# A four-layer graph network on one core: 84 strips of layer 1 are multiplied under layer 0, layer 2's sides are made under layer 1

## The chip, the cores and the metric

The kernel runs on one core of one Trainium2 chip. Its time is the device time of one execution in microseconds. It is written engine by engine: each of TensorE (PE), VectorE (DVE), ScalarE (ACT), GpSimd (POOL) and SyncE (SP, which issues nearly all DMAs) has its own program, runs it in order, and waits for the others by semaphores.

## The reference

Four graph layers over 4096 nodes with 128 features, each followed by a residual sum and a layer norm:

```python
x = _layernorm(x + _L0_gnn_ref(x, adj, W))              # hyperbolic mean: A @ (gamma*XW), A @ (gamma-1), row sums of A
x = _layernorm(x + _L1_gnn_ref(x, adj, W, b))           # D^-1/2 (A+I) D^-1/2 @ x @ W.T + b
x = _layernorm(x + _L2_gnn_ref(t, x, adj, alpha, beta)) # D^-1/2 A D^-1/2 @ x - x
                                                        #   + sigmoid(alpha) * (softmax(beta*cos(x,x)*A) @ x - x)
x = _layernorm(x + _L3_gnn_ref(x, adj, ...))            # relu(A @ x @ W.T + b), then a GRU cell
```

The adjacency A is a dense 4096x4096 fp32 matrix (64 MB), so each layer multiplies it with a matrix of 128 or 129 columns. Layer 2 needs the scores of all pairs of nodes too, with a softmax over each whole row.

## The kernel before, in words

**Tiles.** A is cut into 8 slabs of 512 rows (index s), a slab into 32 strips of 128 columns (index j), two strips make a pair (m, 16 of them), two pairs a group (g, 8 of 1 MB). fp32 products are made of fp16 halves: A's strip and the layer's factor Y are each split in a high and a low part, and three products (high-high, high-low, low-high) are summed in PSUM.

**Layer 0** (`turn0`, `multiply0`, `high0`, `low0`). Each pair of A is loaded in fp32, PE turns it (8 transposes, L525) into one of two strip buffers in PSUM (`strip_a`, `strip_b`), ACT copies the high part (L828), DVE makes the low part (L1352), PE multiplies. Here a quarter strip is the stationary side and Y moves: 130 columns with the low strip (L544), 260 with the high one (L543, L546), for 4 quarters and 2 strips, 16 matmuls a pair. PE turns two pairs ahead of the one that it multiplies, and may turn the next only when the low part of the last but one is made. The split pairs go from a ring of 7 slots back to memory (`adj_t`), from where layers 1 to 3 read them. At a slab's end ACT and DVE read the four sums (`read_acc0`, L834, L835, L1359, L1360), called at pair m == 3 of the next slab. The row work of a slab (`rows0`, some 40 small steps on DVE, ACT and POOL, each waiting for the one before) is spread over the next slab's pairs, steps 2m and 2m+1 at pair m. Layer 1's factor is made from its result (`y_scale` on POOL, `y_high` on ACT, `y_low` on POOL), all in the last slab and behind it.

**Layer 1** (`multiply(1, n)`). The factor is the stationary side and 512 columns of the turned A move, three matmuls of 512 a strip (L567, L568, L574), 6 a pair, 128 pairs in the order of the table TURNS. At a slab's last strip the identity's share, `eye` times a diagonal of 1024, is added (L573). Groups of `adj_t` are loaded into 6 slots in that order. The row work (`rows1`, steps k = 0 to 14, the k-th behind the k-th turn from ROWS_FROM on) ends with x normed to unit length, turned by PE (k == 12) and split into `unit_h`, `unit_l`, the factors of layer 2's scores.

**Layer 2** (`score`, `mask`, `exponentials`, `scale`, `turn2`, `mix`, `multiply2`). A unit is 128 rows by 1024 columns. Its scores take two calls of three matmuls of 512 columns (L612 to L614). A masked product with A and the row's peak take DVE (L1517), which needs the unit of A loaded again from memory (`load_unit`, 25 places in SBUF given by RING). ORDER2 gives the order of units (e = 4 x row block + quarter of the columns). Before slab 0 can be turned (`turn2(0)`, L629), 16 units, the four rows' exponentials on ACT (L897) and their scaling (L903 on ACT, L1549 on DVE) must be done. PEAKS2 and WEIGHTS2 say at which step the first four rows' peaks and weights stand in DVE's program. Two units are multiplied at the end of layer 1, the rest behind it. Units at places from 22 on lie over x (`x_nat`), so their loads wait until Y of layer 2 (`y_high`, `y_low` with L1095 and L1097, and Y_dis, x times a degree factor, L1101) is made for all 8 slabs. **Layer 3** is multiplied like layer 1.

## Time and profile before

| | us |
|---|---|
| three timed runs | 1368.76, 1364.46, 1367.28; median 1367.28 |
| the profiled execution | 1363.03 |
| its span in the trace | 1361.2 |
| PE busy with matmuls | 1245.8 (92%) |
| DVE, ACT, POOL busy | 762.8, 680.2, 483.6 |
| data moved | 413 MB, 303 GB/s over the span |

The page gives busy times per engine and in 40 slices, the chain of waits that ended last, and the costliest groups of instructions. PE's ends are modelled, and weight loads (PEld) lie beside matmuls. A span of PE at 100% in a window means that it waits for nothing; a smaller share has to be read from the timeline.

### The profile page before, as it was taken

What the parts mean: (1) busy time and instruction counts of PE and PEld (TensorE: products, weight loads), DVE (VectorE), ACT (ScalarE), POOL (GpSimd) and SP (SyncE); (2) the same over time, 40 slices, a digit from 0 to 9 for tenths busy, and PEclk for the clock granted to TensorE, in tenths of its full rate; (3) what the DMA queues carried; (4) which work ended last, traced back from release to release, by engine and by line L of the source; (5) the groups of instructions that cost most, each with busy time, mean ns of one, the idle gap of its engine ahead of it and who ended that gap; (6) DMA issues with size and microseconds to landing.
All of it is one profiled execution on the core that took longest, in us unless ns stands there. A gap on an engine that the chain in (4) does not pass through costs nothing.

```text
span 1361.2 us, 20730 instructions
## 1 busy us (share of the span) xinstructions
PE 1245.8 (92%) x7896; PEld 793.4 (58%) x7896; DVE 762.8 (56%) x1716; ACT 680.2 (50%) x983; POOL 483.6 (36%) x459
## 2 busy tenths in 40 slices
PE   5888888888789999986999999999999989999996
PEld 5877777778664555533555555555556554444442
DVE  6755655666551312177778787878878781021223
ACT  5444555445341211154887877887887740112222
POOL 4011221113243321263565666666656571000000
PEclk9899999999899999996999999999999999999998
DMA  9999999999779999936777877778786767987870
GB/s 306 336 415 375 376 387 369 383 386 378 297 279 387 350 362 359 380 139 240 255 263 276 283 275 276 260 262 289 277 284 247 240 245 290 408 309 274 317 283 23
DMA packets 114819, 413.06 MB, mean 303 GB/s; under 512 B 10016, under 2 KB 23584, under 8 KB 90144
## 3 DMA queue, kind: packets, MB, share of 16 engines
q1 hardware_dynamic: 106528, 407.67, 80.7%
q10 hardware_dynamic: 8192, 4.06, 1.0%
q8 instruction: 62, 1.02, 0.3%
q14 instruction: 37, 0.30, 0.1%
HBM read 340.40 MB, written 71.30 MB: 302 GB/s over the span
## 4 chain that ended last, share of the span: by engine, by line
PE 72%; DVE 11%; ACT 6%; POOL 5%; issue 4%; DMA 2%; POOLq 0%; ACTq 0%; DVEq 0%; SPq 0%
PE acc L567 8%; PE acc L568 8%; PE acc L574 8%; PE strip_b L629 8%; PE acc L647 4%; PE acc L644 4%; PE acc L645 4%; PE acc L643 4%; DVE parts L1352 3%; PE strip_b L525 2%; PE strip_a L525 2%; DVE arena L1352 2%; PE strip_a L612 2%; PE strip_a L613 2%; PE strip_a L614 2%
## 5 line engine op out<-in xcount | busy, mean ns | idle before, releaser
L1170 POOL TENSOR_TENSOR parts<-arena,parts 128x512 f16<-128x512 f32 x237 | 275.2, 1170 | 190.0 <-ACT parts L908 186.6
L908 ACT ACTIVATE parts<-arena 128x512 f16<-128x512 f32 x256 | 158.5, 624 | 110.4 <-DVE arena L1558 101.7
L1558 DVE SCALAR_TENSOR_TENSOR arena<-parts,dis,strip_b 128x512 f32<-128x512 f16 x256 | 188.8, 743 | 29.6 <-PE strip_b L629 20.7
L567 PE MATMUL acc<-arena,Y 128*128 128x512 f16 x512 | 194.1, 379 | 3.5 <-DMA arena<-adj_t 2.5
L568 PE MATMUL acc<-arena,Y 128*128 128x512 f16 x512 | 194.1, 379 | 0.0
L574 PE MATMUL acc<-arena,Y 128*128 128x512 f16 x512 | 194.1, 379 | 0.0
L629 PEld LDWEIGHTS strip_b<-ident,arena 128*128 128x128 f32 x1024 | 128.4, 142 | 58.4 <-DVE arena L1558 4.9
L629 PE MATMUL strip_b<-ident,arena 128*128 128x128 f32 x1024 | 155.4, 275 | 7.2 <-ACT arena L903 4.8
L1138 POOL TENSOR_TENSOR sc<-sc,power 128x4 f32<-128x4 f32 x31 | 31.5, 1016 | 324.3 <-DVE sc L1379 324.3
L897 ACT ACTIVATE arena<-arena,neg_peak 128x2048 f32<-128x2048 f32 x64 | 127.3, 1990 | 5.8 <-DVE neg_peak L1528 5.8
L903 ACT ACTIVATE arena<-arena,weight 128x2048 f32<-128x2048 f32 x57 | 113.4, 1989 | 14.0 <-DVE weight L1542 14.0
L1517 DVE CUSTOM_DVE_ANT_0 arena<-strip_a,arena,scal 128x1024 f32<-128x1024 f32 x64 | 82.0, 1281 | 35.1 <-PE strip_a L614 29.3
L647 PE MATMUL acc<-parts,Y 128*128 128x512 f16 x256 | 97.1, 379 | 3.4 <-POOL parts L1170 3.4
L643 PE MATMUL acc<-parts,Y_dis 128*128 128x512 f16 x256 | 97.1, 379 | 0.1
L645 PE MATMUL acc<-parts,Y 128*128 128x512 f16 x256 | 97.0, 379 | 0.0
L644 PE MATMUL acc<-parts,Y 128*128 128x512 f16 x256 | 97.0, 379 | 0.0
L1517 DVE CUSTOM_DVE_ANT_0 arena<-mid,arena,scal 128x1024 f32<-128x1024 f32 x60 | 76.9, 1282 | 35.0 <-PE mid L614 35.0
L525 PE MATMUL strip_a<-ident,arena 128*128 128x128 f32 x512 | 68.9, 279 | 22.6 <-DVE parts L1352 14.4
L567 PEld LDWEIGHTS acc<-arena,Y 128*128 128x128 f16 x512 | 50.1, 98 | 66.5 <-issue 10.2
L568 PEld LDWEIGHTS acc<-arena,Y 128*128 128x128 f16 x512 | 50.1, 98 | 65.4 <-issue 12.6
L525 PE MATMUL strip_b<-ident,arena 128*128 128x128 f32 x512 | 71.2, 284 | 17.3 <-DVE parts L1352 9.8
L574 PEld LDWEIGHTS acc<-arena,Y 128*128 128x128 f16 x512 | 50.1, 98 | 59.5
(321 smaller groups left out, 2398.1 us busy)
## 6 DMA issues: line engine op xcount, KB each, us to landing
arena<-adj_t SPq DMA_DIRECT2D x128, 1024.0 KB, 7.0
arena<-in_adj SPq DMA_DIRECT2D x64, 1024.0 KB, 9.9
arena<-in_adj SPq DMA_DIRECT2D x128, 512.0 KB, 5.7
parts<-adj_t SPq DMA_DIRECT2D x128, 512.0 KB, 6.9
adj_t<-parts SPq DMA_DIRECT2D x37, 1024.0 KB, 8.0
adj_t<-arena SPq DMA_DIRECT2D x27, 1024.0 KB, 8.5
scratch<-v ACTq DMA_DIRECT2D x8, 256.0 KB, 10.4
arena<-scratch SPq DMA_DIRECT2D x8, 256.0 KB, 4.4
```

Source lines behind the costliest of these rows:

```text
L525: last = pe.transpose(strip[n % 2][:, j % 2, P * q:P * (q + 1)], tile[:, j // Q, q, P * (j % Q):P * (j % Q + 1)], ident[:])
L567: pe.matmul(to, Y[:, j, 0:D], high, start=j == 0, stop=False)
L568: pe.matmul(to, Y[:, j, LO:LO + D], high, start=False, stop=False)
L574: last = pe.matmul(to, Y[:, j, 0:D], low, start=False, stop=j == NB - 1)
L629: last = pe.transpose(strip_b[:, b % 2, P * q:P * (q + 1)], unit_in[:, place, P * (j % 8):P * (j % 8 + 1)], ident[:])
L643: pe.matmul(to, Y_dis[:, j, :], kept_slot(b // 2 % KEPT_SLOTS)[:, b % 2, 1, :], start=j == 0, stop=False)
L644: pe.matmul(to, Y[:, j, 0:D], part_h[:, b % 4, :], start=False, stop=False)
L647: pe.matmul(to, Y[:, j, 0:D], part_l[:, b % 4, :], start=False, stop=j == NB - 1).then_inc(product, 1)
L908: act.activation(part_h[:, b % 4, :], mixed[b % G_SLOTS], ACT.Copy).then_inc(high_done, 1)
L1170: pool.tensor_tensor(part_l[:, b % 4, :], mixed[b % G_SLOTS], part_h[:, b % 4, :], ALU.subtract).then_inc(low_done, 1)
L1517: dve.tensor_tensor_reduce(unit_in[:, place, :], flat(scores_at(i)[:]), unit_in[:, place, :], scal[:, 5:6], NEG_HUGE, ALU.mult, ALU.max, p ...
L1558: dve.scalar_tensor_tensor(mixed[b % G_SLOTS], kept_slot(n % KEPT_SLOTS)[:, b % 2, 0, :], dis[:, j:j + 1], strip_b[:, b % 2, :], ALU.mult, ...
```

## The change

1. **Strips ahead.** In layer 0, pair m of slab s is multiplied with layer 1's factor as well when `m // 2 <= s - 2`: 2, 4, ... 12 pairs of slabs 2 to 7, 42 pairs or 84 strips. Y becomes one array of 516 columns: layer 0's low part (0:130) and high part (130:260), layer 1's high (260:388) and low part (388:516). The matmuls of such a pair are 388 and 258 columns wide instead of 260 and 130, and one of 128 is added for each quarter. The additional sums stand in columns 260 to 388 of the same four PSUM banks. `read_acc0` copies them to `turned`, SP stores them (`put_share`, 256 KB a slab) and loads them in layer 1 (`load_share`) over `eye`, where DVE adds the identity's share (`eye_share`, which POOL made before).
2. For that, layer 1's factor of slab s-1 is made at pairs 13 to 15 of slab s. `read_acc0` stands at m == 2, ahead of that pair's split, and the row steps at pair m are 2m+3 and 2m+4.
3. **Layer 1** multiplies the remaining 86 pairs, slabs in the order 0, 1, 6, 7, 4, 5, 2, 3. A slab's row work starts at its end, or 12 turns behind the start of that of the last but one.
4. **Layer 2 under layer 1.** The high part of its factor is made by ACT in each slab's row work, the low part by DVE (`y_low2`). Seven units instead of two are multiplied under layer 1, behind turns 72, 74, ... 84, with the masks at the same steps. ORDER2 takes first the columns whose slabs are done; the last quarter (e % 4 == 1, slabs 2 and 3) comes last, and the peaks of rows 0 to 2 move behind it. Y_dis takes the place of layer 1's high part in Y, so it waits for the end of layer 1.

The core of the diff:

```diff
+Y1H = YW
+Y1L = YW + D
+YC = YW + 2 * D
+YD = YW
+HIGH_AT = [LO, Y1H, 0, 0]
+LOW_AT = [0, Y1L, D, D]
...
+ORDER = {1: [0, 1, 6, 7, 4, 5, 2, 3], 3: list(range(SLABS))}
+FIRST = {1: [2 * max(s - 1, 0) for s in range(SLABS)], 3: [0] * SLABS}
+
+
+def turns(l):
+    return [(s, m) for s in range(2) for m in range(EARLY)] + [(s, m) for s in range(2) for m in range(EARLY, PAIRS)] \
+        + [(s, m) for s in ORDER[l][2:] for m in range(FIRST[l][s], PAIRS)]
+
...
+ENDS1 = [TURNS[1].index((s, PAIRS - 1)) + 1 for s in ORDER[1]]
...
+for at, s in enumerate(ORDER[1]):
+    ROWS_FROM[1][s] = ENDS1[at] if at != 1 else ENDS1[at] + 1
+    if at >= 2:
+        ROWS_FROM[1][s] = max(ENDS1[at], ROWS_FROM[1][ORDER[1][at - 2]] + 12)
+LAST1 = ORDER[1][-1]
...
-ORDER2 = [0, 1, 2, 4, 5, 6, 8, 9, 10, 3, 7, 11, 12, 13, 14, 15] + list(range(16, 4 * NB))
+ORDER2 = [0, 3, 4, 7, 8, 2, 6, 11, 12, 15, 10, 14, 1, 5, 9, 13] + list(range(16, 4 * NB))
+LAST_COLUMNS = 1
...
+EARLY2 = 7
...
-PEAKS2 = {19: 0, 21: 1, 23: 2, 31: 3}
-WEIGHTS2 = {27: 0, 31: 1, 35: 2, 38: 3}
...
+PEAKS2 = {25: 0, 27: 1, 29: 2, 31: 3}
+WEIGHTS2 = {32: 0, 34: 1, 36: 2, 38: 3}
...
+RING = [16, 17, 18, 19, 20, 12, 13, 14, 15, 2, 3, 4, 5, 0, 6, 8, 22, 23, 7, 9, 10, 1, 24, 11, 25]
...
+def early_units(n):
+
+    return [i for i in range(EARLY2) if n == TURNS1 - 14 + 2 * i]
...
+            def put_share(s):
+
+                sp.wait_ge(acc_read, acc_reads_done(0, s))
+                sp.dma_start(share[s], turned[s % 2][:]).then_inc(share_out[s % 2], 16)
+
+            def load_share(s):
+                sp.wait_ge(share_out[s % 2], 16 * (s // 2))
+                sp.wait_ge(product, slab_product(1, two_before1(s)))
+                sp.dma_start(eye[s % 2], share[s]).then_inc(share_in[s % 2], 16)
+
...
+                    if s >= 3 and c == 2:
+                        put_share(s - 1)
...
                 elif place >= 22:
                     sp.wait_ge(y_ready, SLABS * 3)
+                    sp.wait_ge(y_dis_ready, SLABS)
...
+                ahead = m // 2 <= s - 2
+                width = Y1L if ahead else YW
+                if ahead and m % 2 == 0:
+                    pe.wait_ge(y_ready, SLABS + m // 2 + 1)
...
-                            pe.matmul(acc0[q][:, 0:YW], high, Y[:, j, :], start=True, stop=False)
-                        last = pe.matmul(acc0[q][:, 0:LO], low, Y[:, j, 0:LO], start=False, stop=False)
+                            pe.matmul(acc0[q][:, 0:width], high, Y[:, j, 0:width], start=True, stop=False)
+                        last = pe.matmul(acc0[q][:, LO:width], low, Y[:, j, LO:width], start=False, stop=False)
                         if not start:
-                            last = pe.matmul(acc0[q][:, 0:YW], high, Y[:, j, :], start=False, stop=stop)
+                            last = pe.matmul(acc0[q][:, 0:width], high, Y[:, j, 0:width], start=False, stop=stop)
+                        if ahead:
+                            last = pe.matmul(acc0[q][:, Y1H:Y1L], high, Y[:, j, Y1L:YC], start=False, stop=False)
                 last.then_inc(product, 1)
 
...
-                if n in (TURNS_ALL - 4, TURNS_ALL - 2):
-                    for k in range(2):
-                        score(n - (TURNS_ALL - 4) + k)
+                for i in early_units(n):
+                    score(2 * i)
+                    score(2 * i + 1)
+            for n in range(TURNS1, TURNS1 + HOOKS[1]):
+                for k, s in hooks(1, n):
+                    if s != LAST1:
+                        rows1(k, s)
             for n in range(STEPS2):
-                if n == 6:
-                    rows1(2, SLABS - 1)
-                if n == 14:
-                    rows1(12, SLABS - 1)
+                if n == 2 * EARLY2:
+                    rows1(2, LAST1)
+                if n == 23:
+                    rows1(12, LAST1)
...
+                if s >= 2:
+                    if s >= 4:
+                        act.wait_ge(share_out[s % 2], 16 * (s // 2 - 1))
+                    for q in range(2):
+                        last = act.activation(turned[s % 2][:, P * q:P * (q + 1)], acc0[q][:, Y1H:Y1L], ACT.Copy)
+                last.then_inc(acc_read, 1)
...
+                    y_high(2, s)
...
-                if m == 3 and s > 0:
+                if m == 2 and s > 0:
                     read_acc0(s - 1)
                 high0(n)
...
-                    rows0(2 * m, s - 1)
-                    rows0(2 * m + 1, s - 1)
...
+                    rows0(2 * m + 3, s - 1)
+                    rows0(2 * m + 4, s - 1)
+                    if m == 14:
+                        y_high(1, s - 1)
...
+                pool.wait_ge(row[g % 2], row_done(1, g, "ln_out"))
+                pool.wait_ge(product, product_base[2])
+                pool.tensor_tensor(Y[:, rows_, YD:YD + D], x_nat[:, rows_, :], wide(dis_y[:, rows_]),
+                                   ALU.mult).then_inc(y_dis_ready, 1)
...
+                    if m == 13:
+                        y_scale(s - 1)
+                    if m == 15:
+                        y_low(1, s - 1)
...
+            for g in range(GROUPS):
+                y_with_dis(g)
...
-                if 6 <= n < 6 + GROUPS:
-                    y_with_dis(n - 6)
-                    y_low(2, n - 6)
...
+            def y_low2(s):
+                rows_ = slice(Q * s, Q * (s + 1))
+                dve.wait_ge(y_hi, 2 * SLABS + place_in(1, s) + 1)
+                if s == 0:
+                    dve.wait_ge(y_ready, 2 * SLABS)
+                dve.scalar_tensor_tensor(Y[:, rows_, D:2 * D], x_nat[:, rows_, :], Y_SCALE, Y[:, rows_, 0:D],
+                                         ALU.mult, ALU.subtract).then_inc(y_ready, 1)
+
+            def eye_share(s):
+                if place_in(1, s) >= 2:
+                    dve.wait_ge(share_in[s % 2], 16 * (place_in(1, s) // 2))
+                elif s == 0:
+                    dve.wait_ge(row[1], row_done(0, SLABS - 1, "scale"))
+                    dve.tensor_scalar(dcol_a[:], dcol[:], WHOLE, None, ALU.mult).then_inc(dcol_up, 1)
+                    dve.wait_ge(dcol_up, 1)
+                for q in range(Q):
+                    mine, own = Q * s + q, eye[s % 2][:, P * q:P * (q + 1)]
+                    if place_in(1, s) >= 2:
+                        last = dve.scalar_tensor_tensor(own, x_nat[:, mine, :], dcol_a[:, mine:mine + 1], own,
+                                                        ALU.mult, ALU.add)
+                    else:
+                        last = dve.tensor_scalar(own, x_nat[:, mine, :], dcol_a[:, mine:mine + 1], None, ALU.mult)
...
+                if s >= 2:
+                    if s >= 4:
+                        dve.wait_ge(share_out[s % 2], 16 * (s // 2 - 1))
+                    for q in range(2, 4):
+                        last = dve.tensor_copy(turned[s % 2][:, P * q:P * (q + 1)], acc0[q][:, Y1H:Y1L])
+                last.then_inc(acc_read, 1)
...
+            read_acc0(SLABS - 1)
+            for k in range(7, 17):
+                rows0(k, SLABS - 1)
+            eye_share(0)
+            eye_share(1)
+            for k in range(17, 28):
+                rows0(k, SLABS - 1)
...
+                for s in ORDER[1][2:]:
+                    if n == ENDS1[place_in(1, s) - 2] + 3:
+                        eye_share(s)
+                for i in early_units(n):
+                    mask(i)
...
+            for n in range(2 * EARLY2, STEPS2):
+                if n == 2 * EARLY2:
+                    rows1(3, LAST1)
+                    rows1(4, LAST1)
+                if n == 16:
+                    rows1(6, LAST1)
+                if n == 18:
+                    rows1(8, LAST1)
+                if n == 24:
+                    rows1(14, LAST1)
```

In ACT's program, at the start of layer 0's slab 4 (strip_a and strip_b are the turned pairs, acc the sums, turned1 takes the share), the rows before were:

```order
L828 ACTIVATE arena<-strip_a 128x2x512
L828 ACTIVATE arena<-strip_b 128x2x512
L828 ACTIVATE arena<-strip_a 128x2x512
L834 ACTIVATE arena<-acc 128x260
L835 ACTIVATE arena<-acc 128x260
L828 ACTIVATE arena<-strip_b 128x2x512
L828 ACTIVATE arena<-strip_a 128x2x512
L853 ACTIVATE v1,sc1<-t1 128x128 x4
```

and now they are:

```order
L892 ACTIVATE arena<-strip_a 128x2x512
L892 ACTIVATE arena<-strip_b 128x2x512
L898 ACTIVATE arena<-acc 128x260
L899 ACTIVATE arena<-acc 128x260
L904 ACTIVATE turned1<-acc 128x128 x2
L892 ACTIVATE arena<-strip_a 128x2x512
L926 ACTIVATE v1,sc1<-t1 128x128 x4
L892 ACTIVATE arena<-strip_b 128x2x512
L892 ACTIVATE arena<-strip_a 128x2x512
```

Before, the read of the old sums (L834, L835) stood behind the split of the slab's third pair; now it stands ahead of it (L898, L899), with the two copies of the share behind it.

In POOL's program, from the end of layer 1 to the first low part of layer 2 (arena holds x, parts the low parts), the rows before began so, with the last three repeated for eight blocks:

```order
L1164 TENSOR_TENSOR sc<-sc,power 128x4
L1166 TENSOR_TENSOR v<-arena,sc 128x512
L1101 TENSOR_TENSOR Y_dis<-arena,dis_y 128x512
L1095 TENSOR_SCALAR turned<-arena 128x512
L1097 TENSOR_TENSOR Y<-turned,Y 128x4x128
L1101 TENSOR_TENSOR Y_dis<-arena,dis_y 128x512
L1095 TENSOR_SCALAR turned<-arena 128x512
```

and now the whole piece is:

```order
L1201 TENSOR_TENSOR sc<-sc,power 128x4
L1218 TENSOR_TENSOR sc<-sc,power 128x4
L1220 TENSOR_TENSOR v<-arena,sc 128x512
L1163 TENSOR_TENSOR Y<-arena,dis_y 128x4x128 x8
L1224 TENSOR_TENSOR parts<-arena,parts 128x512 x36
```

The eight Y_dis remain, and the scaled copy and the low part of Y are gone from POOL.

In DVE's program, behind the last slab's unit_low (L1509 before, L1586 now; ISA is a mask and the reading of its peak, TENSOR_REDUCE the peak of a row of units), before:

```order
L1517 ISA peak 128x1
L1509 TENSOR_TENSOR arena<-mid,arena 128x512
L1517 ISA arena,peak<-strip_b,arena,scal 128x1024
L1517 ISA peak 128x1
L1517 ISA arena,peak<-strip_a,arena,scal 128x1024
L1517 ISA peak 128x1
L1517 ISA arena,peak<-mid,arena,scal 128x1024
L1517 ISA peak 128x1
L1526 TENSOR_REDUCE row_peak<-peak 128x1
L1528 TENSOR_SCALAR neg_peak<-row_peak 128x1
L1517 ISA arena,peak<-strip_a,arena,scal 128x1024
L1517 ISA peak 128x1
```

and now:

```order
L1594 ISA peak 128x1
L1586 TENSOR_TENSOR arena<-mid,arena 128x512
L1594 ISA arena,peak<-strip_a,arena,scal 128x1024
L1594 ISA peak 128x1
L1603 TENSOR_REDUCE row_peak<-peak 128x1
L1605 TENSOR_SCALAR neg_peak<-row_peak 128x1
L1594 ISA arena,peak<-mid,arena,scal 128x1024
L1594 ISA peak 128x1
L1603 TENSOR_REDUCE row_peak<-peak 128x1
L1605 TENSOR_SCALAR neg_peak<-row_peak 128x1
L1594 ISA arena,peak<-strip_a,arena,scal 128x1024
L1594 ISA peak 128x1
```

Before, three masks (units 7, 8, 9) ran before the first peak, and this stood at unit 9. Now the mask behind unit_low is that of unit 12, the first that needs the last slab's columns, and the peaks of rows 0 to 2 stand behind units 12, 13 and 14.

## Rows read from the trace of the kernel before

**Rows 1.** Windows by stage: busy PE, PEld, DVE, ACT, POOL; clock; DMA; GB/s.
```profile
80.16:125.60 45.44, 38.71 (x384) 35.04 (x385) 26.78 (x66) 22.95 (x42) 7.95 (x10) 0.96 1.03 397
259.90:303.70 43.80, 37.05 (x384) 33.67 (x385) 26.77 (x66) 22.95 (x42) 7.94 (x10) 0.99 1.02 386
353.40:397.40 44.00, 36.95 (x358) 33.51 (x359) 26.72 (x61) 22.43 (x43) 17.75 (x19) 0.92 0.73 283
397.40:583.60 186.20, 185.25 (x934) 94.37 (x933) 38.93 (x180) 28.39 (x70) 50.67 (x50) 1.00 0.96 363
583.60:634.80 51.20, 31.48 (x122) 12.44 (x120) 40.62 (x80) 25.10 (x31) 28.96 (x27) 0.83 0.38 149
```

**Rows 2.** Timeline of PE at a slab's start: start, length, [idle before].
```profile
259.93 0.27 PE L543 MATMUL acc<-Y,arena 128*128 128x260 f16 x1 [3.13 <-DVE arena L1360]
261.26 1.04 PE L525 MATMUL strip_b<-ident,arena 128*128 128x128 f32 x8
263.48 1.04 PE L525 MATMUL strip_a<-ident,arena 128*128 128x128 f32 x8
```

**Rows 3.** Timelines of ACT and of DVE at the same slab's start.
```profile
257.75 0.38 ACT L834 ACTIVATE arena<-acc 128x260 f32<-128x260 f32 x1
...
259.36 0.42 DVE L1360 TENSOR_SCALAR arena<-mid 128x260 f32<-128x260 f32 x1
```

**Rows 4.** Timeline of DVE in one slab, the low splits (L1352), four of sixteen.
```profile
219.60 1.23 DVE L1352 SCALAR_TENSOR_TENSOR arena<-strip_b,arena 128x1024 f16<-128x1024 f32 x1 [4.97 <-ACT arena L828]
...
234.92 1.23 DVE L1352 SCALAR_TENSOR_TENSOR parts<-strip_b,parts 128x1024 f16<-128x1024 f32 x1
...
243.50 1.22 DVE L1352 SCALAR_TENSOR_TENSOR parts<-strip_a,parts 128x1024 f16<-128x1024 f32 x1
...
257.88 1.22 DVE L1352 SCALAR_TENSOR_TENSOR arena<-strip_a,arena 128x1024 f16<-128x1024 f32 x1 [0.99 <-ACT arena L828]
```

**Rows 5.** Timeline of PE at the end of layer 0.
```profile
396.87 0.27 PE L546 MATMUL mid<-Y,parts 128*128 128x260 f16 x1
396.98 0.22 PE L544 MATMUL acc<-Y,parts 128*128 128x130 f16 x1
397.04 0.27 PE L546 MATMUL acc<-Y,parts 128*128 128x260 f16 x1
...
398.76 0.38 PE L567 MATMUL acc<-arena,Y 128*128 128x512 f16 x1 [0.95 <-DVE arena L1360]
398.98 0.38 PE L568 MATMUL acc<-arena,Y 128*128 128x512 f16 x1
```

**Rows 6.** Timelines of POOL and DVE, the last slab's row work.
```profile
593.33 1.04 POOL L1166 TENSOR_TENSOR v<-arena,sc 128x512 f32<-128x512 f32 x1
...
596.74 0.69 DVE L1509 TENSOR_TENSOR arena<-mid,arena 128x512 f16<-128x512 f32 x1
```

**Rows 7.** Timeline of DVE (masks), and two groups of ACT by line.
```profile
601.83 1.28 DVE L1517 CUSTOM_DVE_ANT_0 arena<-strip_a,arena,scal 128x1024 f32<-128x1024 f32 x1
...
603.47 1.28 DVE L1517 CUSTOM_DVE_ANT_0 arena<-mid,arena,scal 128x1024 f32<-128x1024 f32 x1
...
L897 ACT ACTIVATE arena<-arena,neg_peak 128x2048 f32<-128x2048 f32 x64 | 127.3, 1990 | 5.8 <-DVE neg_peak L1528 5.8
...
L828 ACT ACTIVATE parts<-strip_a 128x1024 f16<-128x1024 f32 x37 | 37.6, 1016 | 28.4 <-PE strip_a L525 28.4
```

**Rows 8.** POOL's L1101 by source, then timelines of POOL, DVE and PE.
```profile
L1101 POOL TENSOR_TENSOR Y_dis<-arena,dis_y x8: 1041/1048/2022, 594.3 to 616.1; 128x512 f16<-128x512 f32 x8
...
619.78 1.16 POOL L1097 TENSOR_TENSOR Y<-turned,Y 128x512 f16<-128x512 f32 x1
...
625.01 1.28 DVE L1517 CUSTOM_DVE_ANT_0 arena<-strip_a,arena,scal 128x1024 f32<-128x1024 f32 x1 [5.79 <-DMA arena<-in_adj]
...
628.17 2.48 DVE L1549 TENSOR_SCALAR arena<-arena,weight 128x2048 f32<-128x2048 f32 x2
...
634.79 1.09 PE L629 MATMUL strip_b<-ident,arena 128*128 128x128 f32 x4 [3.58 <-ACT arena L903]
```

More of the change, by code:

```diff
@@ L342, in groups_loaded @@
         def groups_loaded(l, n):
-            before = sum(i % TURNED_SLOTS == n % TURNED_SLOTS for i in range(GROUPS * SLABS)) if l == 3 else 0
+            before = sum(i % TURNED_SLOTS == n % TURNED_SLOTS for i in range(TURNS1 // 2)) if l == 3 else 0
             return 16 * (before + n // TURNED_SLOTS + 1)
@@ L734, in _ @@
                 multiply0(n)
-            for n in range(TURNS_ALL):
+            for n in range(TURNS1):
                 for k, s in hooks(1, n):
@@ L756, in _ @@
                         rows2(m % NB, m // NB - 1)
-            for n in range(TURNS_ALL):
+            for n in range(TURNS3):
                 if n < PAIRS // 2:
@@ L1031, in _ @@
                     y_high(3, (m - 6) % NB // 4)
-            for n in range(TURNS_ALL):
+            for n in range(TURNS3):
                 if n < PAIRS // 2:
@@ L1722, in _ @@
                     rows2(m % NB, m // NB - 1)
-            for n in range(TURNS_ALL):
+            for n in range(TURNS3):
                 if n < PAIRS // 2:
```

236 lines of the change are left out of this document (101 added, 135 removed).

## Prediction

> **What bounds the kernel now.** I read the busy times by stage first [rows 1]. Layer 0 runs to 397.8 us, layer 1 to 583.6, the hand-over into layer 2 to 634.8, and layers 2 and 3 take the rest, which the change leaves as it is apart from places in Y. TensorE (PE) is the engine that all of them have in common, but its limits differ. In layer 1 it is busy for 185.25 of 186.20 us: only fewer matmuls shorten it. In layer 0 a slab lasts 43.8 us or more, and PE has records for 37 of them. In the hand-over PE has 31.5 busy us of 51.2. So I looked next at why PE idles in the last two.
>
> In layer 0 the timeline of PE [rows 2] shows an undisturbed pair: 8 turns and 16 matmuls in 2.22 us (261.26 to 263.48), so 16 pairs are 35.4 us. The other 8.4 us of a 43.8 us slab are in two places. At the slab's start PE waits 3.13 us for the reads of the old sums: ScalarE (ACT) starts its read at 257.75, VectorE (DVE) ends the last of its own at 259.78 [rows 3]. The last product was done a turn (2.22 less 1.33 us of matmuls, 0.9) before PE's wait began at 256.8, so at 255.9. Both engines first wait for the next pair and split it. The rest lies in the row work of the slab before, which holds up the split of strips on DVE, in order. The split of the fourth pair starts at 219.60, that of the third pair of the next slab at 257.88 [rows 4]: 15 pairs in 38.28 us, 5.1 more than 15 times 2.215. By thirds it is 2.0 (219.60 to 234.92, six pairs), 1.9 (to 243.50, three) and 1.1 (to 257.88, six). Slabs of 45.4 us have in addition a stretch at the lower clock behind the 3.13 us wait (granted clock 0.96 in the slab from 80.16, 0.99 in the one from 259.9 [rows 1]). The layer's last matmul ends at 397.81, 0.95 us before layer 1's first [rows 5].
>
> In the hand-over [rows 6 to 8] the last slab's row work takes 13.8 us from 583.6 (unit_low ends at 597.4). Then DVE masks scores at 1.64 us a unit, and from 619.2 it waits: GpSimd (POOL) makes Y_dis and Y's low part for eight blocks until 620.94, only then may units be loaded over x, and DVE goes on at 625.01. Layer 2's first turn is at 634.79.
>
> **Layer 0 after the change.** 42 pairs (84 strips: 2(s-1) pairs of slab s, from 2 to 7) get 384 more moving columns for each of 8 quarter strips. 512 columns go by in 0.215 us (398.76 to 398.98, and over all of layer 1), so this is 0.162 us each, 1.30 us a pair, 54.6 in all. The last matmul of the three has its own weight load and 128 columns. A matmul of 130 columns with its own load takes 0.06 us (396.98 to 397.04 [rows 5]), which is the columns alone, so I add nothing for it. The Trainium skill (TensorE: Matmul & The Clock Gate, Back-to-back issue gap) gives about 81 ns for each matmul of 128 columns in a sustained stream of loads and matmuls, against 54 by columns. By it 336 such matmuls would be 9 us more; the trace does not agree with it, with its 0.06 us.
>
> What hides them: the wait of PE for a strip. Two strip buffers lie between PE and the split, so 1.30 us more of matmuls per pair let DVE fall back 2.6 us before PE feels it. I count a third of the stalls as hidden where its pairs have the added work. Moved by one pair, as the row hooks are, the thirds lie beside products 2 to 6, 7 to 9 and 10 to 12. So hidden are 0, 0, 1.0, 2.0, 2.7, 4.0 and 4.8 us in slabs 1 to 7. The start of a slab: both reads now stand ahead of the next split, as at layer 1's start, where they wait for nothing else and PE idles 0.95 us [rows 5]. The two narrower copies of the share add 0.3 to 0.5, and PE turns a pair meanwhile (0.9). That leaves 0.5 us of the 3.13, and with it goes the stretch at the lower clock. A slab is then 43.8 - 2.6 + 2.6(s-1) - hidden: 41.2, 43.8, 45.4, 47.0, 48.9, 50.2, and 51.5 for the last, which has no start behind it. Slab 0 ends 2.6 us earlier too, at 77.6 instead of 80.16. The seven slabs behind it are 328.0, so layer 0 ends at 405.6 instead of 397.8. For Y1, now made in every slab (two operations of 128x512 on POOL, 1.05 us each by [rows 8], one on ACT), I add 2. Layer 0: +10 us. Bounds: -11 if the 21 us of stalls left go too, +55 if nothing is hidden and the starts stay.
>
> **Layer 1.** 42 pairs of 6 matmuls go: -54.3 us. Ten more score calls of three matmuls come in: +6.5. The transposes of slab 2's unit rows fall behind its end: -0.5; the longer read at its start: +0.5. New waits: the early units' adjacency stands behind the last group in SP's queue, released by product 74 of 86. From release to use one unit took 4.1 us (620.9 to 625.0); with the 1 MB group ahead, at 397 GB/s, 6.7, and the mask 1.3. PE reaches the third early unit 6.1 us after product 74. That is 2 us, and I take 3. Queued behind that mask on DVE are slab 5's unit_low and slab 2's row work, which have four and more turns of slack. The row work now has 12 turns (15.5 us) and the other slab's matmuls, where it takes 10.8 us to the unit on POOL [rows 6], with y_low2 on DVE (0.7, as unit_low of the same size) and the eye share (twice that) added and two slabs interleaved. I take 1 us. The reloads of the share (256 KB) are asked for seven turns ahead (9 us), and DVE needs some 1.4 of these: nothing. The loads need less than before, 43 groups for 64. Layer 1: -44 us, so it ends at about 550 instead of 583.6.
>
> **The hand-over**, from layer 1's end T. Seven units are done instead of two. The row work of the last slab still takes about 14.9 us (13.8 and a mask more between); beneath it go units 7 to 11. Unit 12 needs it: mask at T+16.4, four masks at 1.64 us end at T+23. POOL makes Y_dis alone, 8 times 1.05, from T+10.8: T+19.2, the load 4.1 us more, T+23.3. Y's low part is on DVE under layer 1. Now the exponentials are late: their first row's peak comes at T+18, and eight of 1.99 us [rows 7] end at T+34. On DVE weights and scales (0.7 and 2.5 for a row's two: 628.17 stands 3.16 behind 625.01, two masks and the weights) stand between masks 16, 17 and 18: from T+23, 3.3 + 1.3 + 3.2 + 1.3 + 3.2 + 1.3 + 0.7 and 2.0 for ACT's scale, T+39.5. So the chain over DVE decides, and layer 2's first turn comes after 39.5 instead of 51.2: -12. Bounds: -17, were it the load alone (T+23.3 and the 9.8 us that stood behind it), and 0.
>
> **Sum.** +10 - 44 - 12 = -46. The profiled execution was 1363.0 (span 1361.2 and 1.8 around it), 4.3 below the median of the runs. 1363.0 - 46 + 4.3 = 1321 us. A measurement of this kernel tells 0.3% from no change, 4 us.
>
> **Rivals.**
> The DMA holds layer 0. For: its share is 1.00 and more in slabs at 386 and 397 GB/s [rows 1]. Against: PE waits there for splits, and the longest slabs are now those with most added work. At 397 GB/s 16.8 MB take 42.3 us, so slabs 0 and 1 lose 5 us of their gain and the shares 1: 1327. The Trainium skill (DMA: Bandwidth & Descriptors, Where 436 GB/s comes from) puts HBM's side at about 358 GB/s. By it no slab could be under 46.9 us, and the trace already has 43.8.
>
> Layer 1's row work holds PE. For: eight chains in 56 turns, in pairs 3 turns apart, each engine in order. Against: slack of some 4 us (12 turns of 1.29 and 2.7 of row matmuls, less the 13.8). If two chains go one after the other (27.6 us against 22), PE waits 5.7 us for each of three pairs, 17 in all: 1338.
>
> PE stays at 1.2 GHz in the hand-over. For: its clock was 0.83 there. Nine units at 2.6 us instead of 1.64: +9, 1330.
>
> Short matmuls wait for their weight loads. Against: the 0.06 us of [rows 5]. If each added one took half as long again as its columns (27 ns), 336 of them are 9 us: 1330 too. The skill's figure above would be this case.
>
> The other side: the strip hand-over works one deep. If a pair's turn (0.9), high split (1.0) and low split (1.2) [rows 4, 7] come after, not beside, its matmuls, each of the 42 pairs costs 2.4 us more: +101, 1422, slower. From 1.1 us a pair it decides. Against: with 3.1 us of hand-over the pairs run at 2.22 now, which only two deep allows. And if none of the 54.6 is hidden, the starts stay and layer 2's hand-over keeps its 51 us, the sum is -54 + 6 + 4 + 55 = +11 (1378), slower too, or nothing if half of the starts shrink.
>
> **Chances.** The forecast 0.67, the DMA 0.07, the row work 0.13, the lower clock or slower short matmuls 0.05, no change 0.03, slower 0.05. All but the last two are faster by over 0.3%: 0.92. The range 1307 to 1342 takes in the row work and, below, two thirds of the stalls that I left in layer 0 (21 us).
>
> **What would show it.** In the changed profile: PE's idle before the first matmul of a slab 0.3 to 1 us instead of 3.13; 1.30 us longer pairs at a slab's head and slabs of about 41, 44, 45, 47, 49, 50, 51 us; layer 0's end near 408 us and layer 1's near 550; waits on PE in layer 1 only around the third early unit; DVE not waiting for a load over x after layer 1's end, but on the exponentials or nothing; layer 2's first turn about 40 us after layer 1's end; layers 2 and 3 as long as before (726 us from that turn). It is wrong if slabs 5 to 7 exceed 53 us, or if PE has over 10 us of waits in layer 1.

## The result, and the profile after

The changed kernel takes 1309.22 us (median of 4 runs, 1307.67 to 1312.16), the kernel before 1367.38 beside it (4 runs, 1364.46 to 1368.76): a ratio of 0.958, 95% interval 0.9557 to 0.9603. So 58 us went where 46 were forecast; 1321 was predicted, with a range of 1307 to 1342. The profiled execution is 1309.65 (span 1307.9), against 1363.0 (span 1361.2) before: 53.3 us of span. The other 5 us of the 58 come from the conversion: the kernel before happened to be profiled 4.3 us below its median, the changed one 0.4 above. In experiments that leave the start of the program as it is, the first product of slab 0 stands between 38.2 and 39.9 us, so up to 1.7 us in any difference of two traces is not the kernel's.

The same stages by window, in the profile after (length, then busy time and instructions of PE, PEld, DVE, ACT, POOL; granted clock; DMA share; GB/s), to be read beside [rows 1]: slabs 1, 3, 5 and 7 of layer 0, layer 1, the hand-over.

```profile
75.96:117.57 41.61, 36.66 (x384) 33.67 (x385) 26.73 (x66) 23.57 (x44) 10.17 (x12) 1.00 1.03 416
...
159.75:203.66 43.91, 41.34 (x417) 36.78 (x418) 27.24 (x69) 24.16 (x45) 10.16 (x12) 1.00 1.02 392
...
248.87:296.24 47.37, 46.10 (x448) 39.88 (x449) 27.26 (x69) 24.39 (x45) 10.16 (x12) 1.00 0.98 366
...
346.24:396.32 50.08, 48.74 (x457) 40.35 (x458) 25.04 (x67) 21.42 (x42) 10.16 (x12) 1.00 0.79 300
396.32:542.10 145.78, 139.17 (x703) 72.21 (x704) 57.32 (x227) 30.68 (x73) 42.60 (x41) 0.99 0.85 327
542.10:581.03 38.93, 23.04 (x96) 8.90 (x94) 33.16 (x72) 21.96 (x25) 11.20 (x11) 0.90 0.62 232
```

The eight slabs last 37.5, 41.6, 42.2, 43.9, 45.2, 47.4, 50.0 and 48.7 us. Layer 0's last matmul ends at 395.0 (before at 397.8): it has 42 pairs of added work and is still 2.8 us shorter. Layer 1 lasts 145.8 us instead of 184.8, the hand-over 38.9 instead of 51.2, and from layer 2's first turn to the end it is 726.9 (before 726.4).

A slab's start on PE, which answers to [rows 2]: the last turn of the slab before, then the first product.

```profile
293.94 1.04 PE L580 MATMUL strip_a<-ident,arena 128*128 128x128 f32 x8
296.24 0.32 PE L602 MATMUL acc<-Y,arena 128*128 128x388 f16 x1 [1.27 <-issue]
```

ACT and then DVE at the same start, for [rows 3]:

```profile
294.14 0.39 ACT L898 ACTIVATE arena<-acc 128x260 f32<-128x260 f32 x1 [0.32 <-PE mid L605]
```

```profile
293.85 1.23 DVE L1422 SCALAR_TENSOR_TENSOR arena<-strip_b,arena 128x1024 f16<-128x1024 f32 x1 [0.99 <-ACT arena L892]
295.00 0.42 DVE L1429 TENSOR_SCALAR arena<-mid 128x260 f32<-128x260 f32 x1
...
295.67 0.48 DVE L1435 COPY turned<-mid 128x128 f32<-128x128 f32 x2
```

PE waits 1.27 us instead of 3.13 (0.92 and 0.87 at the starts of slabs 1 and 2, 1.27 at the others). ACT reads as soon as the last product is done, at 294.14. DVE is in the second pair's split until 295.0, and it is the one that ends the wait ("issue" here means that the profile names no releaser; the end of DVE's copies, 296.15, is what fits, and experiment 6 bears it out).

Two more stretches of PE: a pair with the added columns, from its turn to the next (for the 2.22 us of [rows 2] and the 0.06 us of [rows 5]), and the waits inside layer 1 over 0.7 us.

```profile
352.41 1.04 PE L580 MATMUL strip_a<-ident,arena 128*128 128x128 f32 x8
353.29 0.27 PE L603 MATMUL acc<-Y,parts 128*128 128x258 f16 x1
353.40 0.33 PE L605 MATMUL acc<-Y,parts 128*128 128x388 f16 x1
353.57 0.22 PE L607 MATMUL acc<-Y,parts 128*128 128x128 f16 x1
353.63 0.27 PE L603 MATMUL acc<-Y,parts 128*128 128x258 f16 x1
...
355.95 1.04 PE L580 MATMUL strip_b<-ident,arena 128*128 128x128 f32 x8
...
459.96 1.16 PE L646 MATMUL mid<-WT,turned 128*128 128x128 f32 x8 [0.72 <-POOL v L1212]
466.71 1.16 PE L646 MATMUL mid<-WT,turned 128*128 128x128 f32 x8 [1.27 <-POOL v L1212]
482.68 1.16 PE L646 MATMUL mid<-WT,turned 128*128 128x128 f32 x8 [1.82 <-POOL v L1212]
521.29 0.39 PE L671 MATMUL strip_a<-arena 128*128 128x512 f16 x1 [2.79 <-DVE peak L1594]
```

The third matmul, 128 columns with its own weight load, takes 0.06 us (353.57 to 353.63). A pair with added columns takes 3.54 us from turn to turn (352.41 to 355.95), 1.32 more than the 2.22 before; 1.30 was counted.

The hand-over, for [rows 7] and [rows 8]: DVE's mask of unit 12, its mask of unit 18 and the scale behind the fourth weights; ACT's first exponential and last scale; PE's first turn of layer 2.

```profile
558.46 1.28 DVE L1594 CUSTOM_DVE_ANT_0 arena<-strip_a,arena,scal 128x1024 f32<-128x1024 f32 x1 [1.59 <-PE strip_a L673]
...
576.82 1.28 DVE L1594 CUSTOM_DVE_ANT_0 arena<-strip_a,arena,scal 128x1024 f32<-128x1024 f32 x1
...
578.77 1.29 DVE L1626 TENSOR_SCALAR arena<-arena,weight 128x2048 f32<-128x2048 f32 x1
```

```profile
560.17 2.00 ACT L969 ACTIVATE arena<-arena,neg_peak 128x2048 f32<-128x2048 f32 x1 [5.25 <-DVE neg_peak L1605]
...
578.77 2.00 ACT L975 ACTIVATE arena<-arena,weight 128x2048 f32<-128x2048 f32 x1 [2.61 <-DVE weight L1619]
```

```profile
581.03 1.09 PE L688 MATMUL strip_b<-ident,arena 128*128 128x128 f32 x4 [4.48 <-ACT arena L975]
```

With T = 542.1: unit 12's mask at T+16.4, exponentials from T+18.1 to T+34, the first turn at T+38.9. DVE has no wait for a load over x any more.

### The profile page after: what moved, and what is told of

Same layout as the page of the kernel before. It is cut to its first block, busy times and chain, and to the rows that moved or that the text cites. A ratio compares the mean times of both kernels' runs of the same rounds, so it can differ in the third digit from the quotient of the medians.

```text
span 1307.9 us, 20934 instructions
## 1 busy us (share of the span) xinstructions
PE 1227.0 (94%) x7980; PEld 789.5 (60%) x7980; DVE 770.7 (59%) x1769; ACT 685.3 (52%) x995; POOL 460.1 (35%) x433
## 4 chain that ended last, share of the span: by engine, by line
PE 78%; DVE 8%; ACT 5%; DMA 4%; issue 4%; POOL 2%; POOLq 0%; SPq 0%; ACTq 0%; DVEq 0%
PE strip_b L688 8%; PE acc L629 6%; PE acc L630 6%; PE acc L636 6%; PE acc L707 4%; PE acc L705 4%; PE acc L704 4%; PE acc L703 4%; PE acc L605 4%; PE mid L605 4%; PE strip_b L580 3%; PE strip_a L580 3%; PE acc L603 2%; PE mid L603 2%; PE strip_a L671 2%
## 5 line engine op out<-in xcount | busy, mean ns | idle before, releaser
L629 PE MATMUL acc<-arena,Y 128*128 128x512 f16 x428 | 162.8, 380 | 3.5 <-DMA arena<-adj_t 2.0
L688 PE MATMUL strip_b<-ident,arena 128*128 128x128 f32 x1024 | 155.4, 275 | 8.8 <-ACT arena L975 5.7
L630 PE MATMUL acc<-arena,Y 128*128 128x512 f16 x428 | 162.6, 380 | 0.0
L636 PE MATMUL acc<-arena,Y 128*128 128x512 f16 x428 | 162.5, 380 | 0.0
L707 PE MATMUL acc<-parts,Y 128*128 128x512 f16 x256 | 97.1, 379 | 3.4 <-POOL parts L1224 3.4
L703 PE MATMUL acc<-parts,Y 128*128 128x512 f16 x256 | 97.0, 379 | 0.1
L704 PE MATMUL acc<-parts,Y 128*128 128x512 f16 x256 | 97.0, 379 | 0.0
L705 PE MATMUL acc<-parts,Y 128*128 128x512 f16 x256 | 97.0, 379 | 0.0
L629 PEld LDWEIGHTS acc<-arena,Y 128*128 128x128 f16 x428 | 42.0, 98 | 57.4 <-issue 11.4
L630 PEld LDWEIGHTS acc<-arena,Y 128*128 128x128 f16 x428 | 42.0, 98 | 55.8 <-issue 13.1
L1668 DVE SCALAR_TENSOR_TENSOR arena<-arena 128x512 f32<-128x512 f32 x7 | 4.8, 692 | 117.4 <-PE mid L748 87.8
L605 PE MATMUL acc<-Y,parts 128*128 128x260 f16 (+1 forms) x286 | 72.8, 291 | 0.0
## 6 DMA issues: line engine op xcount, KB each, us to landing
scratch<-v ACTq DMA_DIRECT2D x8, 256.0 KB, 10.6
```

The source lines that it names most:

```text
L605: last = pe.matmul(acc0[q][:, 0:width], high, Y[:, j, 0:width], start=False, stop=stop)
L629: pe.matmul(to, y_high, high, start=j == 2 * FIRST[l][s], stop=False)
L630: pe.matmul(to, y_low, high, start=False, stop=False)
L636: last = pe.matmul(to, y_high, low, start=False, stop=j == NB - 1)
L688: last = pe.transpose(strip_b[:, b % 2, P * q:P * (q + 1)], unit_in[:, place, P * (j % 8):P * (j % 8 + 1)], ident[:])
L703: pe.matmul(to, Y[:, j, YD:YD + D], kept_slot(b // 2 % KEPT_SLOTS)[:, b % 2, 1, :], start=j == 0, stop=False)
```

## Experiments

All ratios are to the kernel before, measured beside it, with their 95% intervals; "the changed kernel" is 0.958 (0.9557 to 0.9603).

**1. The reads alone.** The kernel before, with the read of the old sums a pair earlier on ACT and DVE and the row hooks behind it.

```diff
-                if m == 3 and s > 0:
+                if m == 2 and s > 0:
                     read_acc0(s - 1)
...
-                    rows0(2 * m, s - 1)
-                    rows0(2 * m + 1, s - 1)
+                    rows0(2 * m + 3, s - 1)
+                    rows0(2 * m + 4, s - 1)
```

> The kernel before with one thing changed: the old sums of a slab are read ahead of the split of its third pair (instead of the fourth), and the row hooks stand a turn earlier. Theory A (the forecast's): TensorE's idle at seven slab starts falls from 3.13 us to 0.5 to 0.9, 16 to 18 us in all, and the stretches at the lower clock behind it go, 1.6 us in four slabs: 1344 us (1340 to 1350). Rival B: the split that now stands behind the reads comes late instead, and TensorE waits for that: 1362 to 1367.

1336.18 us, ratio 0.9763 (0.9738 to 0.9789). Its profile, PE at a slab's start, then that slab by window:

```profile
119.49 0.27 PE L543 MATMUL acc<-Y,parts 128*128 128x260 f16 x1 [0.92 <-DVE arena L1360]
```

```profile
77.85:119.49 41.64, 36.67 (x384) 33.68 (x385) 26.73 (x66) 23.07 (x43) 7.96 (x10) 1.00 1.03 416
```

The idle is 0.92 in all seven starts, slab 1's clock is 1.00 where it was 0.96 [rows 1], and slabs 1 to 6 are 41.6 to 42.6 us instead of 43.8 to 49.7. Layer 1 starts at 372.5 instead of 398.8, 26 us earlier. Rival B is refuted: PE's waits for splits up to layer 1 are 37.6 us, where they were 39.1. Theory A has the direction and the 0.9 us, but the time lies below its range of 1340 to 1350. The seven starts give 7 times 2.21, 15.5 us. Most of what theory A lacks is slab 6, 49.7 us before and 42.2 now. DVE and POOL in that slab of the kernel before, with the same DVE step in slab 5 first, and PE's wait that follows:

```profile
292.70 1.12 DVE L1386 TENSOR_SCALAR arena<-t,sc 128x128 f32<-128x128 f32 x4
...
338.59 3.28 DVE L1386 TENSOR_SCALAR arena<-t,sc 128x128 f32<-128x128 f32 x4
```

```profile
337.50 4.03 POOL L1085 TENSOR_TENSOR arena<-arena,dcol_y 128x512 f32<-128x512 f32 x4
```

```profile
343.15 1.23 PE L525 MATMUL strip_a<-ident,arena 128*128 128x128 f32 x8 [3.10 <-DVE arena L1352]
```

Beside POOL's products DVE's four scalings take 3.28 us instead of 1.12, the split queued behind them is late, and PE waits 3.10 us, with the clock at 0.94 over the slab. In this experiment the scalings take 1.79 us there and that wait is gone. So part of the 26 us comes from where the row steps now lie and not from PE's wait for the reads; no run moves the reads without the row hooks. The forecast took this slab for one of 43.8 us.

**2. The added columns left out.**

```diff
-                width = Y1L if ahead else YW
+                width = YW
...
-                        if ahead:
-                            last = pe.matmul(acc0[q][:, Y1H:Y1L], high, Y[:, j, Y1L:YC], start=False, stop=False)
```

> The changed kernel without the 384 added columns of layer 0's 84 strips (but for one matmul in each bank that opens it); layer 1 still leaves those strips out, so the kernel computes less than the reference. Theory A (TensorE alone sets slabs 5 to 7 of the changed kernel; the stalls come back where the columns go): all slabs as slab 1, 41.6 us, the last 39: layer 0 ends about 366 instead of 395, and the time is 1280 us. Forecast's term (only 14.5 of 54.6 us lie in stalls): 40 us less than the changed kernel, 1269. Rival (transfers set the slabs at about 41.6): as A in time, but the wait in a slab is then for the loaded tile and not for the split.

1282.61 us, ratio 0.9369 (0.9346 to 0.9392). Slabs 2 and 6 of it by window:

```profile
119.50:161.53 42.03, 36.86 (x384) 33.67 (x385) 27.23 (x69) 24.02 (x46) 10.15 (x12) 1.00 1.03 415
...
287.52:330.18 42.66, 38.14 (x384) 35.05 (x385) 27.17 (x69) 23.94 (x45) 10.14 (x12) 0.96 1.02 401
```

Without the columns slabs 1 to 6 last 41.6 to 42.7 us, and from slab 1's first product to layer 1's it is 291.4 us (77.9 to 369.3) instead of 320.4 (76.0 to 396.3): 29.0 less. The columns are 42 times 1.32, 55.4 us, of PE's time: 26.4 of them lay in stalls, nearly twice the 14.5 of the forecast. About 3 of the 26.4 are PE at the lower clock in slabs 3 and 6 (PE busy for 38.1 us there, clock 0.96, where slab 1 has 36.7 us at 1.00), the rest are waits. Theory A holds; the forecast's term falls. The waits inside the slabs are for DVE's splits in both kernels, none for a loaded tile. The first long stall in slab 2 is back, which the changed kernel has only in slab 1:

```profile
130.19 1.06 PE L580 MATMUL strip_a<-ident,arena 128*128 128x128 f32 x8 [1.99 <-DVE arena L1421]
```

**3. Two early units instead of seven.** `EARLY2 = 2`.

> The changed kernel with two score units under layer 1 instead of seven. Theory A (five units cost layer 1 6.5 us of matmuls and the 2.8 us wait at the third; in the hand-over they lie beside row work for the most part): layer 1 ends 9.3 us earlier, the mask of unit 12 comes at T+22 instead of T+16.4: 1306 us. Rival B (the units cost nothing in layer 1 and the whole 8.2 us of five masks comes back in the hand-over): 1317.

1309.19 us, ratio 0.957 (0.9547 to 0.9593): no difference to the changed kernel that can be measured. Layer 1 is 9.1 us shorter (136.7 us from 397.7 to 534.4, for 145.8), as theory A has it. But the hand-over is not 5.6 us longer, it is 12.3: its window, and DVE's mask of unit 12.

```profile
534.40:585.60 51.20, 32.76 (x125) 13.21 (x125) 40.27 (x83) 22.72 (x27) 14.60 (x14) 0.86 0.53 206
```

```profile
562.32 1.28 DVE L1594 CUSTOM_DVE_ANT_0 arena<-strip_a,arena,scal 128x1024 f32<-128x1024 f32 x1 [2.23 <-PE strip_a L673]
```

The mask stands at T+27.9, not T+22. Six masks, 8.2 us (542.9 to 551.1), where the changed kernel has one, now stand between two steps of the last slab's row work on DVE, which executes in order: they lengthen the row work instead of lying beside it. That row work also starts later, 5.9 us after layer 1's end for 2.0. Both theories missed. The five units are paid in layer 1 and returned in the hand-over: in total time they are worth nothing here. The 3 us more in the trace are those of an execution that took 1313.4, 4.2 above the median. The row steps keep the places that suit seven units; a version with two units and the steps moved ahead of the masks was not run, so it is not shown that 51 us is the least that two units allow.

**4. Layer 1 in plain order.** Two places follow from the order and are not printed: two more turns of row hooks behind layer 1, and a bound on where the share is loaded.

```diff
-ORDER = {1: [0, 1, 6, 7, 4, 5, 2, 3], 3: list(range(SLABS))}
+ORDER = {1: list(range(SLABS)), 3: list(range(SLABS))}
...
-ORDER2 = [0, 3, 4, 7, 8, 2, 6, 11, 12, 15, 10, 14, 1, 5, 9, 13] + list(range(16, 4 * NB))
+ORDER2 = [0, 1, 4, 5, 8, 9, 12, 13, 2, 6, 10, 14, 3, 7, 11, 15] + list(range(16, 4 * NB))
-LAST_COLUMNS = 1
+LAST_COLUMNS = 3
```

> The changed kernel with layer 1's slabs in the order 0 to 7, and the score units in an order that fits it (the columns of slabs 0 to 3 first, those of 6 and 7 last). Theory A: slabs 6 and 7, with 6 and 4 turns, end 5.2 us apart, so slab 6's row work (13.8 us) reaches 8.6 us past layer 1's end and slab 7's starts behind it: unit 12 is masked at T+25 instead of T+16.4, 1318 us. Rival B: the order is worth nothing, since exponentials and scales set the hand-over: 1309.

1320.73 us, ratio 0.9647 (0.9622 to 0.9671), 11.5 us over the changed kernel. PE in its hand-over (T = 544.7):

```profile
552.44 1.12 PE L654 MATMUL mid<-ident,v 128*128 128x128 f32 x4 [7.23 <-POOL v L1220]
...
593.60 1.08 PE L688 MATMUL strip_b<-ident,arena 128*128 128x128 f32 x4 [5.75 <-ACT arena L975]
```

The first turn is at T+48.9 (a mask at T+25 would put it at T+47.5; it stands at T+26.1), because slab 6's unit rows come 7.7 us after the layer's end, with slab 7's row work behind them. That is 10 of the 11.5 us, as theory A has it. Layer 1 itself is 1 us longer, from two changes that nearly cancel: PE waits 7.05 us at the third early unit instead of 2.79, and 0.7 us for row work instead of 3.8.

**5. The low part back on GpSimd.** In `y_with_dis`, behind Y_dis, with DVE's `y_low2` taken out:

```diff
+                pool.tensor_scalar(source, x_nat[:, rows_, :], Y_SCALE, 0.0, ALU.mult, ALU.add)
+                pool.tensor_tensor(Y[:, rows_, D:2 * D], source, Y[:, rows_, 0:D], ALU.subtract)
```

> The changed kernel with the low part of layer 2's Y made on GpSimd behind Y_dis (two operations a block, as before the change) instead of on VectorE under layer 1; the seven early units stay. Theory A (the gain of the hand-over needs both the x sides and the early units, the later of the two chains decides): GpSimd ends Y_dis at T+18.5 and the low parts 16.8 us later, the loads over x land at T+39.4, VectorE masks unit 16 then instead of at T+26, and layer 2's first turn comes at T+52: 1322 us. Rival B (the early units made the whole gain, as the run with two of them suggests, where the hand-over took 51.2 us although the x sides were early): the turn stays near T+39, 1309.

1318.61 us, ratio 0.9631 (0.9611 to 0.9652). DVE, and PE's first turn (T = 540.9):

```profile
564.74 3.79 DVE L1631 TENSOR_SCALAR arena<-arena,weight 128x2048 f32<-128x2048 f32 x2
579.55 1.28 DVE L1599 CUSTOM_DVE_ANT_0 arena<-strip_a,arena,scal 128x1024 f32<-128x1024 f32 x1 [11.02 <-DMA arena<-in_adj]
```

```profile
592.48 1.08 PE L689 MATMUL strip_b<-ident,arena 128*128 128x128 f32 x4 [4.48 <-ACT arena L976]
```

The load over x ends at T+38.7 (T+39.4 expected) and the turn is at T+51.6 (T+52): theory A. Layer 1 is 2.7 us shorter (143.1), which was not expected, so the low part on DVE is not free there, and 9.4 us of the hand-over's 12.7 reach the total. With experiment 3: either one put back alone makes the hand-over 51 us again. For the x sides the wait of 11.02 us shows why; for the early units it holds with the row steps where they are.

**6 to 9. Three waits taken out of the changed kernel,** each alone and then together: in DVE's loop of layer 0 the reads ahead of the second pair's split; in SyncE's the loads of nine units between groups; the fourth row's weights ahead of unit 18's mask.

```diff
-                if m == 2 and s > 0:
+                if m == 1 and s > 0:
                     read_acc0(s - 1)
```
```diff
                 load_group(1, n)
+                if 0 <= n - 33 < 9:
+                    load_unit(n - 33)
```
```diff
-WEIGHTS2 = {32: 0, 34: 1, 36: 2, 38: 3}
+WEIGHTS2 = {32: [0], 34: [1], 36: [2, 3]}
```

> The changed kernel with VectorE's reads of the old sums ahead of the split of the slab's second pair (ScalarE's stay ahead of the third). Theory A (the 1.27 us at a slab's start is VectorE ending the second pair's split first: the last product is done at 294.1, its reads start at 295.0): the idle falls to 0.4 us in six slabs, 5 us less than the changed kernel: 1304. Rival B (the second pair's split, now later, holds TensorE's turns): no gain, 1309.

1302.99 us, ratio 0.9534 (0.9512 to 0.9555). The idle at the starts of slabs 3 to 7 is 0.42 us, slabs 3 to 6 are 0.84 shorter each, and layer 1 starts 4.7 us earlier. Theory A. In slabs 1 and 2 rival B has its share: the starts have no idle over 0.1 us, PE waits 0.8 more for later splits, and the slabs are as long as before.

> The changed kernel with the loads of the first nine score units issued between the last ten groups of layer 1 instead of behind them. Theory A (the 2.79 us wait of TensorE at the third early unit is the place of the unit loads in SyncE's queue): that wait goes and layer 1 is 2.8 us shorter, with nothing given back in the hand-over: 1306.4. Rival B (the groups behind the units come late, or the hand-over is set by something that does not move with layer 1's end): 1309.

1306.72 us, ratio 0.9559 (0.9538 to 0.958). PE's wait at the third early unit is gone, and with it the lower clock behind it. First the changed kernel from 520 us to layer 1's end, then this one:

```profile
520.00:542.00 22.00, 20.71 (x92) 9.70 (x93) 13.19 (x33) 2.27 (x5) 4.60 (x4) 0.92 0.62 250
```

```profile
520.00:537.00 17.00, 17.00 (x84) 8.29 (x83) 10.23 (x28) 2.28 (x5) 4.74 (x4) 1.00 0.48 194
```

Layer 1 is 4.9 us shorter, not 2.8; in this execution the hand-over took 1.3 back (40.2 us), and the total is 2.5 us less, about the wait itself.

> The changed kernel with the weights of the fourth block row computed ahead of the mask of unit 18 instead of behind it. Theory A (layer 2's first turn waits for the last exponential, these weights and ScalarE's scale): the first turn comes 1.2 us earlier, 37.7 us after layer 1's end: 1308. Rival B (the mask that now stands behind holds the next turns or the first mixes): the turn comes earlier and the gain is gone by the third one: 1309.2.

1307.76 us, ratio 0.9564 (0.9542 to 0.9586). The time alone would not tell it from the changed kernel. The trace does: the first turn stands at T+37.7, as theory A has it.

```profile
579.80 0.45 PE L688 MATMUL strip_b<-ident,arena 128*128 128x128 f32 x1 [4.55 <-ACT arena L975]
```

> The changed kernel with all three edits: VectorE's reads ahead of the second pair's split, the loads of nine units between layer 1's groups, the fourth row's weights ahead of unit 18's mask. Theory A (they touch different stages and add up): 5 + 2.8 + 1.2 = 9 us less than the changed kernel, 1300. Rival B: what one stage gives, a later one takes back: 1304 to 1309.

1298.86 us, ratio 0.9501 (0.948 to 0.9522). They add up: 10.4 us less than the changed kernel.

**10. The row hooks of layer 0 spread,** on top of the three. The stall that remains in slab 1 of the changed kernel is this, on ACT:

```profile
75.08 1.02 ACT L892 ACTIVATE parts<-strip_a 128x1024 f16<-128x1024 f32 x1 [0.21 <-PE strip_a L580]
78.68 0.31 ACT L926 ACTIVATE v<-t 128x128 f32<-128x128 f32 x1 [2.58 <-DVE sc L1490]
...
79.87 1.00 ACT L892 ACTIVATE parts<-strip_b 128x1024 f16<-128x1024 f32 x1
```

ACT stands 2.58 us at a step of the row work whose input DVE has not made yet, with the next pair's split (79.87) queued behind; DVE in turn waits 2.25 us for that split.

```diff
+ACT_ROWS = {3: [8], 6: [13], 8: [18], 9: [19], 11: [21]}
+DVE_ROWS = {2: [7, 8], 3: [9], 5: [10, 11, 12], 7: [14, 15, 16, 17], 10: [20], 12: [22], 13: [24], 14: [27]}
...
-                    rows0(2 * m + 3, s - 1)
-                    rows0(2 * m + 4, s - 1)
+                    for k in ACT_ROWS.get(m, []):
+                        rows0(k, s - 1)
...
```

DVE's loop takes its steps from `DVE_ROWS` in the same way, and ACT makes the high part of layer 1's factor at pair 15 instead of 14.

> The kernel with the three edits together (1298.9 us), and in layer 0 the row hooks of ScalarE and VectorE a pair or two behind the work they wait for, spread over pairs 2 to 15 instead of 2 to 14 in twos. Theory A (what is left of the stalls in slabs 1 to 4, 9 us of waits for the split, comes from ScalarE and VectorE standing at a row step whose input is not there, with a split queued behind it): 6 us less, 1293. Rival B (the splits are late because the two engines have as much work, not because they wait, or Y1 now comes late for the next slab's head): 1299 or more.

1290.97 us, ratio 0.9437 (0.9417 to 0.9456): 7.9 us less than with the three edits, 18 less than the changed kernel. Slabs 1 and 4 by window:

```profile
76.58:113.13 36.55, 35.98 (x384) 33.74 (x385) 27.25 (x67) 23.54 (x43) 10.15 (x12) 1.00 1.03 415
...
194.38:238.93 44.55, 43.98 (x433) 38.32 (x433) 27.60 (x69) 24.14 (x45) 10.14 (x12) 1.00 1.03 415
```

Slab 1 falls from 41.6 us to 36.55, with PE busy for 35.98 of them; DVE and ACT do the same work as before. So the 5 us in slab 1 were engines standing in order at a row step, and not a lack of time. Slabs 2 and 3 give 2.7 and 1.1 us; slabs 4 to 6 are 0.2 to 0.7 longer than with the three edits (no run shows why), and PE waits 0.48 us at the last turn of each of slabs 1 to 6. No first product of slabs 1 to 7 waits over 0.1 us any more.

## Why the forecast came out as it did

The direction, the order of the terms and most mechanisms were right; the time was 12 us too high. It would have been 17 without luck: layer 1 gained 5 us less than forecast, which hid part of the 12.6 by which layer 0 did better and the 4.3 of the conversion. By its steps:

**Layer 0, forecast +10, measured -2.8: the term that was mis-sized.** The price of the columns was right (1.32 us a pair for 1.30). The removal of the start's idle was right in kind, and its 0.5 us too low (0.9 to 1.3). Wrong was "I count a third of the stalls as hidden where its pairs have the added work". PE's own time sets a floor of 35.4 us for a slab, plus 2.64 for each two pairs with added columns. What was above the floor in slabs 1 to 6 is 6.2, 4.1, 3.2, 1.9, 1.4 and 1.4 us; the forecast had left 5.8, 5.7, 4.7, 3.7, 2.9 and 1.6. Two pairs at a slab's head already take away 2.1 us in slab 2, because the first long stall, 10.6 us into the slab, comes right behind them (that DVE catches up meanwhile fits, but no run isolates it), and from slab 5 on there is nothing left but the start. Experiment 2 gives the sum: 26.4 us hidden for 14.5. The base was uneven too: the forecast gave every slab 43.8 us, where four of the seven before took 45.2 to 45.5 and slab 6 took 49.7; it named the lower clock for the four, and not the 5.9 us of slab 6 (experiment 1). They went with the change, so no error came of it. Two smaller things in this term were wrong as well. The last slab has no turns for three of its pairs, 3 times 0.88 us, which the 51.5 us left out (measured 48.7, all of it PE). And the 2 us for Y1 were not there: it lies beside other work. The 12.6 us between 407.6 and 395.0 are then 6.2 in slabs 1 to 6, 2.8 in slab 7, 2.0 for Y1, and 1.6 up to slab 1's first product, of which 1.0 is the program's start (38.45 for 39.46), which the change does not touch.

**Layer 1, forecast -44, measured -39.0.** The matmuls are as counted. Waits were 3 for the third early unit (2.79) and 1 for the row work (3.8, three waits for the x that GpSimd adds the bias to), 2.8 too low. Not in the sum at all was the lower clock behind the 2.79 us wait: 0.92 over 22 us, 1.8 us. The kernel with the units' loads earlier took 4.9 us off the layer, the wait and the clock together.

**The hand-over, forecast -12, measured -12.3,** and its inner times too (unit 12's mask T+16.4 for T+16.4, masks' end T+22.6 for T+23, Y_dis T+18.5 for T+19.2, exponentials T+34 for T+34, the turn T+38.9 for T+39.5). That the chain over DVE decides is what experiment 8 (the weights earlier) confirmed: 1.2 us off that chain moved the turn by 1.2.

**The conversion.** The sum was made in the profiled time (1317) and 4.3 us were added to get a median. The changed kernel's executions lie closer together (1307.7 to 1312.2; the kernel before 1363.2 to 1372.3 over the experiments), and its profile is no outlier. The slower executions of the kernel before have the lower mean granted clock (1372.3 at 0.968, 1363.2 at 0.974); that the slab starts make it fits, but was not tested.

**The rivals.** The DMA as a floor: refuted, slabs moved 416 GB/s where 397 had been the most, and PE had no wait for a tile. The Trainium skill (DMA: Bandwidth & Descriptors, Where 436 GB/s comes from) has 358 GB/s for HBM's side, by which no slab could be under 46.9 us; slab 1 took 41.6, and the trace decides. The same page (Measured (HBM→SBUF, 128 partitions, SWDGE, issued from GpSimd)) gives the 358 as each core's part when both cores of an HBM domain stream, and here one core runs; the prediction left this condition out. Short matmuls bound by their weight loads: refuted by 0.06 us and by pairs of 3.54, where the Trainium skill (TensorE: Matmul & The Clock Gate, Back-to-back issue gap) has about 81 ns. The row work in layer 1: 3.8 us, not 17. The lower clock in the hand-over: there (0.90), but already in the times from which the chain was worked out. The strip hand-over one deep: refuted, pairs run at 3.54.

## What to carry to other kernels

An engine that waits now and then has room for work, but how much is hidden is not the share of the stalls that lies beside it: give each stretch a floor by the bottleneck's own busy time and take the maximum of the floor and what the other engines need. Here that rule would be the greater of 41.6 us and the floor with its 1.4 us of start: 41.6, 41.6, 42.1, 44.7, 47.4 and 50.0 for slabs 1 to 6, measured 41.6, 42.2, 43.9, 45.2, 47.4 and 50.0. So it is a lower bound, up to 1.8 us short where the two are close. In an engine that executes in order, a step whose input is still being made costs what is queued behind it; moving such steps one or two pairs back was worth 8 us here for no work saved, and moving one read ahead of one split, with the row steps behind it, 26 in the trace. Where two chains end together, a change that shortens one alone shows nothing in that stage (experiments 3 and 5), so undo both singly before you call either useless. Then look at the total: the early units shorten the hand-over and lengthen layer 1 by about as much.
